# Restoring the batch layout of a half with sixteen 32 by 32 tiles instead of two steps of 128-row matmuls

## The reference, cut to what matters

```python
x = x + dilated_attention(group_norm(x))      # first layer
x = x + channel_attention(group_norm(x))      # second layer
```

## Time and profile before

| | |
|---|---|
| median of 3 runs | 84.35 us (84.25 to 84.52) |
| profiled execution | 84.39 us |
| its span, first to last instruction | 82.6 us |
| TensorE matmuls busy | 67.3 us, 888 instructions |
| VectorE busy | 69.6 us |
| GpSimd busy | 42.4 us |
| ScalarE busy | 30.7 us |

### The profile page before, as it was taken

How to read it: one execution, slowest core, us unless ns; L and a number is a source line. 1 busy time by engine, 2 the same in 40 slices (tenths; PEclk the granted TensorE clock), 3 DMA queues, 4 the chain that set the end, 5 groups by cost and what they waited for, 6 DMA issues and landing times.

```text
span 82.6 us, 2228 instructions
## 1 busy us (share of the span) xinstructions
PE 67.3 (81%) x888; PEld 49.0 (59%) x888; DVE 69.6 (84%) x191; ACT 30.7 (37%) x97; POOL 42.4 (51%) x82
## 2 busy tenths in 40 slices
PE   0099899799867979999966797979999787999960
PEld 0099695476433656686855664667685545677830
DVE  1087679999999999999999698889999999857980
ACT  4396599615537000000030004220993155485320
POOL 7104279108700009999999999899990003300000
PEclk9999999999999999999999999999999999999999
DMA  0995004000000000000000000000000000011244
GB/s 5 315 356 150 1 0 100 5 0 0 8 0 0 4 12 0 0 0 0 12 0 0 0 0 0 0 8 0 0 0 0 0 8 4 0 63 64 71 158 159
DMA packets 3019, 3.11 MB, mean 38 GB/s; under 512 B 320, under 2 KB 2752, under 8 KB 3008
## 3 DMA queue, kind: packets, MB, share of 16 engines
q1 hardware_dynamic: 2576, 2.69, 9.9%
q10 hardware_dynamic: 432, 0.26, 1.4%
HBM read 1.91 MB, written 1.05 MB: 36 GB/s over the span
## 4 chain that ended last, share of the span: by engine, by line
DVE 42%; POOL 29%; PE 13%; issue 5%; DMA 4%; ACT 2%; POOLq 1%; ACTq 0%
DVE qk L572 17%; POOL acc L340 13%; POOL pv L340 12%; PE ps L763 11%; DVE pv L613 5%; DMA xt<-x_dram 4%; POOL rstd L305 4%; DVE acc L625 4%; DVE pv L625 3%; DVE x L632 2%; PE ps L898 2%; DVE ssum L589 1%; ACT pT L402 1%; DVE x L658 1%; POOLq L99 1%
## 5 line engine op out<-in xcount | busy, mean ns | idle before, releaser
L763 PE MATMUL ps<-prob,sel 64*128 64x192 f32 (+6 forms) x192 | 17.7, 313 | 2.9 <-DVE pv L613 1.9
L613 DVE TENSOR_TENSOR pv<-ps,v 128x128 f32<-128x128 f32 (+7 forms) x32 | 17.1, 569 | 1.7 <-PE ps L763 0.9
L763 PE MATMUL ps<-xn,wp 128*32 128x256 f32 (+1 forms) x208 | 16.4, 382 | 1.7 <-DVE shifted L582 1.2
L763 PEld LDWEIGHTS ps<-prob,sel 64*128 64x128 f32 x192 | 13.7, 186 | 6.9 <-DVE pv L613 4.8
L340 POOL TENSOR_TENSOR pv<-pv 128x240 f32<-128x240 f32 (+3 forms) x24 | 14.6, 617 | 0.1
L572 DVE TENSOR_TENSOR qk<-q,k 128x720 f32<-128x720 f32 (+7 forms) x24 | 13.9, 646 | 0.1
L763 PE MATMUL ps<-xt 128*128 128x128 f32 x56 | 10.6, 334 | 4.1 <-DMA xt<-x_dram 4.1
L763 PEld LDWEIGHTS ps<-xn,wp 128*32 128x32 f32 (+1 forms) x208 | 9.7, 116 | 6.3 <-DVE shifted L582 1.7
L340 POOL TENSOR_TENSOR acc<-acc,pv 128x256 f32<-128x256 f32 (+4 forms) x20 | 12.6, 635 | 0.5
L305 POOL TENSOR_TENSOR rstd<-gvar,mhalf 128x2 f32<-128x2 f32 (+1 forms) x6 | 4.9, 824 | 14.9 <-DVE gvar L516 14.9
L763 PEld LDWEIGHTS ps<-xt 128*128 128x128 f32 x56 | 8.6, 230 | 5.2 <-DMA xt<-x_dram 4.1
(11 more groups left out here) (75 smaller groups left out, 94.0 us busy)
## 6 DMA issues: line engine op xcount, KB each, us to landing
xt<-x_dram SPq DMA_DIRECT2D x4, 256.0 KB, 3.6
out_dram<-x SPq DMA_DIRECT2D x8, 128.0 KB, 1.8
wp<-wpack_dram SPq DMA_DIRECT2D x1, 325.0 KB, 5.6
sel<-selc_dram SPq DMA_DIRECT2D x4, 64.0 KB, 3.9
cs<-consts_dram ACTq DMA_DIRECT2D x1, 130.0 KB, 3.3
cs<-consts_dram ACTq DMA_DIRECT2D x2, 64.0 KB, 2.6
```

What stands on the lines that cost most here:

```text
L613: last = nc.vector.tensor_tensor(o, a, b, ALU.mult)
L763: return nc.tensor.matmul(o, w, m, start=start, stop=stop)
```

## The change

`restore(g)` of a group becomes `restore(ph)` of a half. It is called once where `restore(0)` stood and once where `restore(2)` stood; the calls `restore(1)` and `restore(3)` go away. It takes the 32 partitions of a slot as the rows of the matmul, with a 32 x 32 block of the identity, and writes the four batches' banks (`BANK[2 * ph]` to `BANK[2 * ph] + 3`). The number of `mm` in a half stays 16. The dilation is now the outer loop and the batch the inner one; the four batches raise `restored` with their last dilation. `restore(0)` waits for both softmax shifts, since it now writes banks 6 and 7 as well. Nothing else in any engine's list changes.

```diff
-            def restore(g):
-
-                ph, first = g // 2, GB * (g % 2)
-                if g % 2 == 0:
-                    pe.wait_ge(added, ADDS * sum(POOL_SUMS[:ph + 1]))
-                    if POOL_SUMS[ph] < ND:
-                        pe.wait_ge(dve_added, ADDS * (ND - POOL_SUMS[ph]))
+            def restore(ph):
+
+                pe.wait_ge(added, ADDS * sum(POOL_SUMS[:ph + 1]))
                 if ph == 0:
-                    pe.wait_ge(shift_ready, g + 1)
+                    pe.wait_ge(shift_ready, PHASES)
                     pe.wait_ge(qk_ready, ND * PHASES)
-                if g == 2:
+                else:
+                    pe.wait_ge(dve_added, ADDS * (ND - POOL_SUMS[ph]))
                     pe.wait_ge(pv_ready, 12 * PHASES)
-                for i in range(GB):
-                    for s in range(ND):
-                        last = mm(ps[32 * s:32 * s + 32, BANK[g] + i, 0:N],
-                                  ident[:, 32 * (first + i):32 * (first + i) + 32], acc[:, ph, s, :])
-                    last.then_inc(restored, 1)
+                for s in range(ND):
+                    for j in range(SLOTS):
+                        rows = slice(32 * j, 32 * j + 32)
+                        last = mm(ps[32 * s:32 * s + 32, BANK[2 * ph] + j, 0:N], ident[rows, rows], acc[rows, ph, s, :])
+                        if s == ND - 1:
+                            last.then_inc(restored, 1)
 
@@ -969,7 +967,6 @@
             restore(0)
             spread(1, 1, 1)
             group_stats(0)
-            restore(1)
             spread(1, 1, 2)
             group_stats(1)
             for i in range(2):
@@ -992,8 +989,7 @@
             attention(1)
             pe.wait_ge(pv_ready, 12 * PHASES)
             keep_clock(3, BANK[2])
-            restore(2)
-            restore(3)
+            restore(1)
             fuse(0, 0)
             group_stats(2)
             finish(0, 0)
```

## The result

The changed kernel takes 87.44 us (median of 4 executions, 87.01 to 87.80) against 84.44 us for the kernel before, measured beside it (84.25 to 84.55). The ratio is 1.0356 with a 95% interval of 1.0302 to 1.0409. The forecast was 84.4 us with a range of 83.9 to 85.9, so it was wrong. Ratios in this document are taken over the executions within 1.5% of the fastest of their kernel, which can leave out some in which the clock fell longest; medians and ranges are of all.

The account below looks back on a forecast made before the run. The prediction took VectorE and GpSimd, not TensorE's matmuls, to bound the kernel. Half 0 at 0 plus half 1 at 0.06 us, on the profiled 84.39 us, gave a median of 84.4 us, range 83.9 to 85.9.

Parts of the forecast that it names:

- rival 2: TensorE's clock falls after half 1 and slows the `finish` steps: 1.5 us more, 85.9; chance 0.20.
- In half 0 there is more cover.: Half 0: a clock fall there would meet more slack than one after half 1; no size given.
- The price: Kernel's end, at low clock: 14 `finish` MATMULs after 71.1 lose 0.215 us each, 3.0 if all; half taken, 1.5.
- The tiles run together: Restore of each half: all 16 tiles work at once, 32 MATMULs done in 0.72 us.
- rival 1: Both restores: tiles don't all run together; 86.3 us in the worst form, 85.4 in the milder; chance 0.16, time 85.4.
- Half 0 gains nothing: Half 0: VectorE's waits of 0.25 and 0.32 us before the products go, but `gst` waits for squares; gain 0.
- The cover behind it: Half 0, GpSimd: an earlier `gst` would not help, as `gsq` takes 0.34 us and `rstd` follows it at 52.90.
- Half 1 costs 0.06: Half 1: the first batch is ready 0.06 us later, so VectorE's residual starts later and this reaches the end.
- the sum: Whole kernel: 0 from half 0 plus 0.06 us from half 1 on 84.39 us; median forecast 84.4; chance 0.50.
- Rival 3: Half 0: `gst` and what follows up to 0.57 us earlier, or `gvar` freed; 83.8 to 84.1; chance 0.14, time 84.0.

Follow-up runs that it names:

- the filled kernel: The changed kernel plus 4 dummy matmuls in half 0 and 6 behind half 1's restore: 84.73 us, ratio 1.0015 to the kernel before.
- the merge: Changed kernel with dummies; half 0 takes both residuals in a row, with one statistics matmul, variance and power for four batches: 84.18 us, ratio 0.9929.
- the merged kernel with the old restores: The kernel before with half 0's residuals, statistics, variance and power put together, keeping its 128-row restores, the second behind the first spread: 86.54 us, no ratio.
- half 1 filled: The changed kernel plus only the 6 dummy matmuls behind the restore of half 1: 86.39 us, ratio 1.0117 to the kernel before.
- thin work: The kernel before with its old 128-row restores, each matmul 64 columns wide instead of 256, that quarter read four times: 87.41 us, ratio 1.0229.
- half the fill: The changed kernel plus 2 dummy matmuls in half 0 and 3 in half 1: 85.44 us, ratio 1.0055 to the kernel before.

## Why the prediction was wrong

**The step that failed is rival 2, "the clock falls".** It named the mechanism, the place in half 1, the idle time (1.6 us forecast, 1.69 measured), and then gave it 0.20 and one fall of 1.5 us. There were two, worth 1.9 and 1.2 us, and the forecast of 84.4 had the clock at nothing: "Granted clock 1.00 after 49".

- *"In half 0 there is more cover."* This was the costlier error. The prediction worked out that VectorE and GpSimd would not gain in half 0, and was right, and took this for a statement about TensorE's clock too. But half 0 lost its array time as half 1 did, 0.43 us left of 1.7, and there every spread after the fall feeds VectorE. The low stretch lasted 6.8 us and moved half 1's start by 1.89.
- *"Against: the page's row of the granted clock shows no slice below full."* That row is of the kernel with the work still in it. It says that the amount of then was enough and nothing about less. The dummies that stand all over TensorE's list were the better evidence, and they were given too little weight.
- *The price.* Half of 14 slow matmuls of `finish` gave 1.5 us. The measured second fall cost 1.2, but that it came out near is luck. The low stretch, from about 72.4 to 75.9, met six matmuls of `project_second`, two of `finish` and three of `fuse`, and twelve of the sixteen of `finish` ran after it at full clock:

```profile
L763 PE MATMUL ps<-xn,wp 128*128 128x256 f32 x6 | 2.6, 605 | 0.0
L763 PE MATMUL ps<-p,mT 128*128 128x256 f32 x2 | 1.2, 713 | 0.0
L763 PE MATMUL ps<-p,mT 128*128 128x256 f32 x12 | 3.2, 388 | 0.1
```

**What held.** The other steps are in the trace nearly as written. The tiles run together: 0.73 and 0.71 us against a forecast of 0.72, so rival 1 is out in both its forms. Half 0 gains nothing: residual at 50.19, products at 50.87 and 53.42 without a wait, `gst` again at 52.09 and 54.64, `rstd` at 52.90. The cover behind it was read right as well, `gsq` takes 0.33 again. Half 1 costs 0.06 up to `asum`, which is the size of the forecast, but two errors cancel in it. The residual starts 0.15 late rather than 0.06, since VectorE goes on 0.14 us after the burst's recorded end (68.25 after 68.11) and not 0.04. And 0.09 come back, since the second batch is there with the first; the prediction had counted no gap between the two residuals. `fuse(0, 0)` has the idle time that TensorE saved. With the clock held the sum comes out: the filled kernel's ratio is 1.0015 (0.9962 to 1.0068), and its profiled execution took 84.48 us where the sum said 84.45.

**Rival 3** (the VectorE waits are worth something) did not happen by itself. It took the merge, another change of order, to gain 0.7%, and how much of that is the saved waits is not shown.

## What to carry to other kernels

Matmul work that looks idle on the chain may be what holds TensorE's clock. When an edit makes it cheaper, put dummies into the idle time that it opens, at every place that it thins and not only the last; here 4 and 6 held the clock in ten of ten executions, 2 and 3 in four of thirteen. Look at the clock of several executions: one that never falls in the profile is no proof of a margin, and of the 90 executions of the kernel before that stand beside the experiments three show 0.98. And when a transfer between layouts becomes one short burst, look for what can be merged behind it: the burst alone gained nothing here.

## What the runs showed of the hardware

- The granted clock fell although TensorE never stood idle for long: the longest waits ahead of the first fall are 0.89 and 1.42 us, ahead of the second 1.69; one of 0.68 stands ahead of the fall in the merged kernel with the old restores, and one of 1.20 in the kernel before at full clock. The Trainium skill (TensorE: Matmul & The Clock Gate, Why this matters for your kernels) asks for no idle gaps above about 3 us; here shorter gaps between short bursts were enough, and the measurement decides.
- The low stretches had different lengths, 6.8 us (55.4 to 62.2) and 3.3 us or a little more (72.5 to 75.8) in one execution, and 10 us in the kernels with half 1 filled and with thin work, where TensorE was busy throughout. And the same program can fall in one execution and not in the next (four of thirteen held with half the fill).
- Sixteen 32 by 32 tiles do run together in fp32, with two passes each: 32 matmuls of 256 columns in 0.71 to 0.73 us, where four tiles at a time took 1.93. The Trainium skill (TensorE: Matmul & The Clock Gate, Part 3) says of 16 tiles that they run together, and the trace agrees.
- The waiting engine sees the result of such a burst 0.11 to 0.16 us after its recorded end (66.31 and 67.04 after ends at 66.20 and 66.88), where it took 0.03 after the statistics matmuls. Fewer increments did not shorten it.
